# Third graph layer on one core: a block of weights kept in building order and turned by strided columns

## The reference, cut to what matters

```python
h = jnp.maximum(_layernorm(x, axis=-1), 0.0)
# edge_index = stack([src, dst]); here the first row is the destination
msgs = edge_values[:, None] * h[edge_index[1]]
AX = jax.ops.segment_sum(msgs, edge_index[0], num_segments=6250)
x = x + jnp.einsum('nd,od->no', AX, W) + b
```

## Time and profile before

| what | us |
|---|---|
| median of 3 runs | 6583.97 (6581.0 to 6584.98) |
| the profiled execution, its own time | 6582.25 |
| its span in the trace | 6580.7 |
| mean granted TensorE clock over the span | 0.939 of full |

### The profile page before, as it was taken

The page is one execution under the profiler, slowest core; times in us unless marked ns, Lnnn a source line. Parts: engine busy times, 40 slices in busy tenths (PEclk is TensorE's granted clock), DMA queues, the critical chain, the costliest instruction groups (busy, mean ns, idle before and its releaser), DMA issues.

```text
span 6580.7 us, 115387 instructions
## 1 busy us (share of the span) xinstructions
PE 5741.6 (87%) x44199; PEld 3832.5 (58%) x44199; DVE 3735.5 (57%) x6004; ACT 2828.1 (43%) x5343; POOL 2065.4 (31%) x2152
## 2 busy tenths in 40 slices
PE   1199999599999898999998599999999999969997
PEld 0177776255555555555555366666666666646665
DVE  4688887333333333333333699999999999930001
ACT  0155555344444444444444355555555555500001
POOL 3101110077777777777776000000000000001110
PEclk6599999799999999999999799999999999959998
DMA  5245454144444454444444000000000000016664
GB/s 172 68 177 181 173 185 156 56 109 113 112 111 111 111 113 111 111 110 111 110 110 121 29 4 4 4 4 4 4 4 4 4 4 4 3 50 204 204 204 132
DMA packets 551872, 593.21 MB, mean 90 GB/s; under 512 B 299789, under 2 KB 475758, under 8 KB 531422
## 3 DMA queue, kind: packets, MB, share of 16 engines
q1 hardware_dynamic: 461103, 433.29, 21.3%
q0 software_dynamic: 87488, 151.98, 10.8%
q10 hardware_dynamic: 2738, 0.54, 0.0%
HBM read 361.67 MB, written 204.48 MB: 86 GB/s over the span
## 4 chain that ended last, share of the span: by engine, by line
PE 37%; DVE 22%; POOL 22%; issue 13%; DMA 3%; ACT 1%; SPq 1%; DVEq 0%; POOLq 0%; ACTq 0%
PE psum L1199 33%; POOL H L690 11%; POOL G L690 10%; DVE R L716 9%; DVE HT L716 5%; DVE l L716 4%; DMA H<-gather_table,cols_pc 1%; PE psum L1456 1%; DVE cols_pc L716 1%; PE psum L1406 1%; DMA G<-gather_table,cols_pc 1%; PE psum L1408 1%; POOL R L657 1%; DVE lns L722 1%; POOL ACC L650 1%
## 5 line engine op out<-in xcount | busy, mean ns | idle before, releaser
L1520 ACT ACTIVATE R<-psum 128x512 f32<-128x512 f32 (+3 forms) x2482 | 1314.4, 556 | 1443.6 <-PE psum L1408 919.6
L1199 PE MATMUL psum<-R,l 128*128 128x512 f32 (+2 forms) x2826 | 1460.5, 598 | 66.1 <-DVE HT L716 63.6
L1199 PE MATMUL psum<-R,HT 128*128 128x384 bf16 x6076 | 1084.7, 326 | 59.8 <-DVEq L1188 59.8
L1199 PEld LDWEIGHTS psum<-R,G 128*128 128x128 bf16 x11840 | 733.9, 98 | 567.5 <-issue 334.0
L1199 PE MATMUL psum<-R 128*128 128x98 bf16 (+3 forms) x6858 | 997.4, 284 | 62.5 <-DVE R L716 40.0
L690 POOL DMA_INDIRECT G<-gather_table,cols_pc x908 | 867.6, 955 | 425.1 <-issue 271.9
L690 POOL DMA_INDIRECT H<-gather_table,cols_pc x896 | 856.5, 956 | 273.1 <-issue 263.9
L1520 ACT ACTIVATE H<-psum 128x392 f32<-128x392 f32 (+1 forms) x1056 | 570.8, 541 | 686.3 <-PE psum L1199 461.9
L1199 PE MATMUL psum<-R,G 128*128 128x98 bf16 x11840 | 811.6, 208 | 44.9 <-DVE R L716 31.1
L1199 PEld LDWEIGHTS psum<-R,HT 128*128 128x128 bf16 x6076 | 566.9, 97 | 383.8 <-DVEq L1188 60.1
L1094 DVE CUSTOM_DVE_ANT_0 R<-psum,R,att 128x512 f32<-128x512 f32 x451 | 338.3, 750 | 794.6 <-PE psum L1199 793.5
(11 more groups left out here) (228 smaller groups left out, 6931.8 us busy)
## 6 DMA issues: line engine op xcount, KB each, us to landing
adjacency_blocks<-HT SPq DMA_DIRECT2D x74, 1568.0 KB, 5.4
HT<-adjacency_blocks SPq DMA_DIRECT2D x50, 1568.0 KB, 6.6
H<-local_dst_pairs SPq DMA_DIRECT2D x113, 512.0 KB
R<-adjacency_blocks SPq DMA_DIRECT2D x24, 1568.0 KB, 6.6
attention_sums<-H SPq DMA_DIRECT2D x451, 69.5 KB, 2.2
R<-ACC SPq DMA_DIRECT2D x451, 64.0 KB
G<-gather_table,cols_pc POOLq DMA_INDIRECT x908
H<-gather_table,cols_pc POOLq DMA_INDIRECT x896
```

Of the source, the lines that this page charges most:

```text
L1199: return nc.tensor.matmul(o, lhs_t, rhs, start=start, stop=stop)
L1520: return nc.scalar.activation(o, a, f, **kw)
```

## The change

`BW` is viewed as (c w) where it was viewed as (w c): the 49 windows of one column lie side by side now, and the columns stand 49 numbers (196 bytes) apart. ACT writes the 4 x 98 results of a unit just as they lie in PSUM, as one run of 392 numbers. PE transposes, for window w, the 128 numbers `BW[:, :, w]` of each partition, every 49th number. Nothing else is changed: the same instructions in the same number and order, the same buffers, the same waits.

```diff
@@ line 270
-        BW = [o[:, 0:NP].rearrange("p (w c) -> p w c", w=W) for o in (r1, hflat)]
+        BW = [o[:, 0:NP].rearrange("p (c w) -> p c w", w=W) for o in (r1, hflat)]
@@ line 1456, turn, on PE
-                    last_ins = nc.tensor.transpose(bank4(3 + n % 2)[:, j, :], BW[b % 2][:, w0_ + j, :], ident[:, :])
+                    last_ins = nc.tensor.transpose(bank4(3 + n % 2)[:, j, :], BW[b % 2][:, :, w0_ + j], ident[:, :])
@@ line 1655, copy_weighted, on ACT
-                activation(BW[b % 2][:, :, 8 * u:8 * u + 8].rearrange("p w (q d) -> p w q d", d=2),
-                           units.rearrange("p q (d w) -> p w q d", d=2), ACT.Copy).then_inc(s_we, 1)
+                activation(BW[b % 2][:, 8 * u:8 * u + 8, :].rearrange("p (q d) w -> p q (d w)", d=2), units, ACT.Copy).then_inc(s_we, 1)
```

## The result

The changed kernel takes 6615.41 us (median of 5, 6610.54 to 6621.01), the kernel before 6583.97 us beside it (median of 5): a ratio of 1.0048, 95% interval 1.0033 to 1.0062. That is 31 us or half a per cent slower, inside the range, but not the 6591 us that was called likeliest. It has the sign of the mild form of the first rival (6629 us) and two thirds of its size.

What follows compares the result with a forecast made beforehand. PE and DVE, both 95% busy and tied by waits, were taken as the bound; 74 blocks x 0.106 us gave +8 us, ACT 0, on 6582.25 us, so 6591 us after rounding, range 6578 to 6860 us.

Steps and rivals of the forecast that it cites:

- the mild form of the first rival: Transpose loads in `turn`: at 133 ns a load outlasts the 111 ns between matmuls; +45 us, 6629 us; chance 0.22.
- What bounds: Third layer's loop: PE and DVE each 95% busy, tied by waits both ways; a block takes 27.34 us.
- ACT's part: ACT's 128x392 copy per unit: plain saves at most 2 ns of 497, taken as 0.
- the size of the load's price: PE's strided weight load: doubles from 53 to 106 ns, still fitting into the 111 ns between matmuls.
- the cover: Quarters outside the PE piece: 0.16 us of extra load time disappears inside 0.33 us of slack.
- The PE piece: PE's 5.03 us stretch of a block's round: two full transpose groups lie in it, adding 0.106 us per block.
- The exposed first load: First load of each transpose group: its matmul waits for it, so each group pays 53 ns once.
- The load as the bound of the transposes: Rival 1, loads in `turn` above 111 ns set the pace: slower; chance 0.22 mild, 0.28 dear.
- the fourfold load: Rival 1's dear form, transpose loads of 213 ns: +250 to +275 us, about 6845 us; chance 0.28.
- The free stride: Rival 2, PE's transpose loads: the stride costs nothing, every row as before, 6583 us; chance 0.20.
- The gain by a plain copy: Rival 3, ACT's copy before a block's first turn: ends 0.1 us earlier, 7 us gained, 6576 us; chance 0.04.
- the refused form of instruction: Rival 4, LDWEIGHTS: strided operand refused a fast form and loaded another way, priced as rival 1; chance inside rival 1's.

Runs made afterwards that it cites:

- the run of that half alone: Changed kernel with ScalarE's plain copy kept but TensorE transposing adjacent numbers: 7391.74 us against 7392.85 for the kernel before, ratio 0.9999.
- the run at 32 apart: Changed kernel with TensorE reading every 32nd number instead of every 49th: 6598.57 us (single execution) beside 6581.94 for the kernel before.
- the run of TensorE's half: Kernel before, ScalarE still reordering, with TensorE reading every 49th number: 7423.59 us, ratio 1.0040 to the kernel before.

## Why the prediction was right or wrong

The measured 6615 us lies in the range of 6578 to 6860 us, but outside the forecast's own 6580 to 6600 and on the side of a rival. The mechanism was right in kind: a strided load is slower, PE pays at the first load of a group, and waits cover a part of it. Two terms of the sum were wrong, and they are the steps that failed.

**What bounds.** Right: two engines tied by waits, so that the path of a block runs through DVE and PE in turn.

**ACT's part.** Right: 0 was taken, 1 ns in the row and 0.9999 in the run of that half alone.

**First step that failed, the size of the load's price:** "I take the doubling, 106 ns". The record grew by 77 ns at the median, to 218 ns where the forecast said 194 and the rival's mild form 220. So loading takes about 53 + 77 = 130 ns, an estimate, and the 0.123 us between transposes of a group says about the same. That is the one number per ns which the DVE row proved, and which I had called an upper bound for the mild case. It was the nearest row, and the better choice. At 106 ns a load just fits behind its matmul, as the run at 32 apart shows; at 130 ns it does not. The prediction named its own sign of being wrong, a distance between transposes beyond 111 ns, and that sign came: 0.107 us before by the same reckoning as above, 0.123 after.

**Second step that failed, the cover:** "3 x 0.053 = 0.16 us, inside the cover of 0.33 us". There is no such cover in the second quarter of a block. I took it as the difference between a quarter of DVE (6.47 us) and PE's own work in one (6.14). But PE starts its quarter only when DVE's last table is done, 0.15 us after DVE has opened the next quarter (4533.92 - 4533.77), and DVE starts 0.74 us after PE began the last build, which itself takes 0.56. From release to release PE's part is 6.36 us and nothing is in hand. In the changed kernel the three groups of that quarter add 0.32 us in full, more than two thirds of the loss; at 32 apart, with the very load that the forecast took, they add 0.17.

**The PE piece, right by luck.** The sum had it grow by two groups of 0.053 us, 0.106. From the send at 4514.38 to DVE's start at 4519.52 it is 5.14 us for 5.03, so it grew by 0.11. But the path enters this piece later than I had it, at the send that DVE's second addition releases, and only one full group lies behind that send. One group of 0.11 us gives the same number as two of 0.053. With the right price for a load, my two groups would have given 0.22.

**The exposed first load** is there: 0.06 us of a group's 0.11, by the lone transpose (0.13 us to its send before, 0.19 after). It doesn't show between the load's start and the matmul's (0.04 us before, 0.05 after), but behind the matmul's start. The rival's mild form put a group at 0.146 us and a block at 0.6; a group costs 0.11 and a block 0.46.

**Rivals.** The load as the bound of the transposes is what happened, mildly (0.22 of the chances); the fourfold load, 0.28, did not. The free stride (0.20) is refuted by the run of TensorE's half. The gain by a plain copy and the refused form of instruction did not occur: counts and forms are equal. The event with 0.50, slower by over 0.2%, came, but the single number went with the band of no change.

**The arguments for 0.** DVE's and ACT's free strides did not carry over to this load. The load takes in adjacent numbers more than twice as fast as they do (0.4 ns a number against 0.85 for ACT and about 1 for DVE); that this is the reason was argued and not tested.

## What to carry to other kernels

A float32 slice that TensorE transposes is read by the weight load, and of the seven distances tried here that load was fast only for adjacent numbers; let ScalarE reorder while it copies out of PSUM, where it cost 497 ns against 498 plain. When two engines are 95% full and wait for each other, follow the path from release to release, with the start and end of each wait, and count which pieces of work lie on it. The difference between two engines' busy times is not cover: 0.33 us of it stood here on paper for each quarter, and in one quarter there was none. Before trimming a wait in such a round, look for the next one behind it and for pairs of dependent instructions whose gap the moved instruction was filling.

## What the runs showed of the hardware that was not expected

- A float32 LDWEIGHTS of 128 columns for a transpose: 140 ns adjacent, 207 ns at every 2nd number, 209 at every 4th, 193 and 194 at every 32nd and 48th, 217 and 218 at every 33rd and 49th. Why the multiples of 16 are cheaper than 2 or 4 wasn't tried further.
- The matmul of a lone transpose starts 0.04 to 0.05 us after its load starts at either distance. The longer load shows behind that start: the next matmul comes 0.13 us after it with adjacent numbers, 0.19 us with every 49th.
- DVE: behind a bf16 instruction that writes 1568 numbers, the next one starts 1.00 us later if it reads them (with a semaphore wait for them), and 0.88 or 0.89 us later if it doesn't.
